# Last sparse feed-forward: paced scatters and gathers, earlier routing, expert tiles two shared batches later

## The reference, cut to what matters

```python
    def _L3_ffn_ref(x, w12, w3, router_w, expert_bias, sw1, sw2, sw3):
        g = x @ sw1.T
        u = x @ sw2.T
        shared_out = jax.nn.silu(g) * u @ sw3.T
        scores = jax.nn.sigmoid(x @ router_w.T)
        selection_scores = scores + expert_bias
        _, top_idx = jax.lax.top_k(selection_scores, TOPK)
        top_scores = jnp.take_along_axis(scores, top_idx, axis=-1)
        top_scores = top_scores / (top_scores.sum(-1, keepdims=True) + 1e-09)
...
        combine = jnp.zeros((T, E), x.dtype).at[jnp.arange(T)[:, None], flat_idx].add(flat_sc)
        h12 = jnp.einsum('td,ehd->teh', flat_x, w12)
        h1, h2 = jnp.split(h12, 2, axis=-1)
        h = jax.nn.silu(h1) * h2
        out_e = jnp.einsum('teh,edh->ted', h, w3)
        routed_out = jnp.einsum('ted,te->td', out_e, combine).reshape(b, s, d)
        return shared_out + routed_out
...
    x = x + jnp.tanh(g_ffn[3]) * _L3_ffn_ref(_layernorm(x, axis=-1), L3_ffn_w12, L3_ffn_w3, L3_ffn_router_w, L3_ffn_expert_bias, L3_ffn_sw1, L3_ffn_sw2, L3_ffn_sw3)
```

## Time and profile before

| | |
|---|---|
| timed runs | 2801.77, 2791.93, 2798.63 us; median 2798.63 us |
| profiled execution, its own time | 2822.25 us |
| span of its trace | 2820.5 us |
| mean granted TensorE clock | 0.933 of full speed |
| PE busy | 2371.5 us, 84% of the span |
| DVE, ACT, POOL busy | 1440.5, 1060.3, 602.9 us |

### The profile page before, as it was taken

One profiled execution on the slowest core, in us unless ns is written; L12 is line 12 of the kernel. 1 busy time (PEld: TensorE's weight loads), 2 busy tenths in 40 slices (PEclk: granted clock), 3 DMA queues, 4 the chain that ended last, 5 costly groups with the idle time before them and its releaser, 6 DMA issues. The chain is left out here.

```text
span 2820.5 us, 38098 instructions
## 1 busy us (share of the span) xinstructions
PE 2371.5 (84%) x10857; PEld 1472.6 (52%) x10884; DVE 1440.5 (51%) x3533; ACT 1060.3 (38%) x3280; POOL 602.9 (21%) x846
## 2 busy tenths in 40 slices
PE   4959999999788868868999999999444488877899
PEld 2436776677555434435666666666222255535675
DVE  4961111111245567745666566666577567762233
ACT  1022222122145435545555555555222255541232
POOL 3702222222123300003333333332000000003012
PEclk8959999999999989989999999999766699989999
DMA  7000000000300000000000000000200000021142
GB/s 286 0 7 6 6 6 6 6 6 6 130 5 0 0 3 0 0 6 1 1 0 0 0 0 0 0 0 0 106 0 0 3 5 4 4 76 47 58 128 64
DMA packets 40625, 68.83 MB, mean 24 GB/s; under 512 B 6752, under 2 KB 34400, under 8 KB 39264
## 3 DMA queue, kind: packets, MB, share of 16 engines
q1 hardware_dynamic: 37472, 59.44, 6.0%
q0 software_dynamic: 3072, 8.39, 0.9%
HBM read 51.30 MB, written 16.52 MB: 24 GB/s over the span
## 5 line engine op out<-in xcount | busy, mean ns | idle before, releaser
L808 DVE TENSOR_TENSOR moe_hid<-moe_act_g,moe_pU 128x384 f32<-128x384 f32 x128 | 70.9, 554 | 443.4 <-ACT moe_act_g L780 443.4
L780 ACT ACTIVATE moe_act_g<-moe_pG 128x384 f32<-128x384 f32 x128 | 62.8, 490 | 424.5 <-PE moe_pU L735 424.5
L714 POOL TENSOR_TENSOR moe_hidw<-moe_hid,moe_data_w_all 128x384 f32<-128x384 f32 x128 | 105.7, 826 | 426.7 <-DVE moe_hid L808 419.9
L1939 ACT ACTIVATE l2x_prob<-l2x_pS,l2x_nb,l2x_rms_q 128x256 f32<-128x256 f32 x256 | 142.5, 565 | 133.4 <-DVE l2x_nb L2087 133.4
L735 PE MATMUL moe_pG<-big,moe_xT 128*128 128x384 f32 x512 | 187.5, 489 | 4.1 <-POOL moe_xT L702 4.1
L756 PE MATMUL moe_pO<-big,moe_hT 128*128 128x256 f32 x768 | 186.8, 379 | 0.0
L735 PE MATMUL moe_pU<-big,moe_xT 128*128 128x384 f32 x512 | 186.3, 487 | 0.0
L967 PE MATMUL l2x_pQ<-big,l2x_xT 128*128 128x512 f32 x320 | 155.0, 607 | 13.7 <-POOL l2x_cT L2016 10.9
L756 PEld LDWEIGHTS moe_pO<-big,moe_hT 128*128 128x128 f32 x768 | 136.0, 190 | 13.2
L2084 DVE TENSOR_REDUCE l2x_negmax<-l2x_pS 128x2 f32<-128x512 f32 x128 | 87.8, 686 | 98.1 <-PE l2x_pS L1828 95.3
L735 PEld LDWEIGHTS moe_pU<-big,moe_xT 128*128 128x128 f32 x512 | 97.6, 191 | 68.3 <-issue 0.9
(11 more groups left out here) (454 smaller groups left out, 5230.4 us busy)
## 6 DMA issues: line engine op xcount, KB each, us to landing
route_x<-l3f_zero SPq DMA_DIRECT2D x1, 4992.0 KB, 16.7
l3f_xg<-route_x SPq DMA_DIRECT2D x39, 128.0 KB, 2.2
route_y<-l3f_y SPq DMA_DIRECT2D x39, 128.0 KB, 1.7
big<-in_f_gu SPq DMA_DIRECT2D x1, 4096.0 KB, 14.9
big<-in_e_gate SPq DMA_DIRECT2D x1, 3072.0 KB, 19.9
big<-in_e_up SPq DMA_DIRECT2D x1, 3072.0 KB, 20.6
big<-in_e_down SPq DMA_DIRECT2D x1, 3072.0 KB, 27.5
moe_lanes<-in_l2f_lanes SPq DMA_DIRECT2D x16, 192.0 KB, 2.8
```

The costliest lines, as they stand in the source:

```text
L714: pool.tensor_tensor(hidw[c % 2][:].rearrange("p (e i) -> p e i", e=n), hid[c % 2][:].rearrange("p (e i) -> p e i", e=n), bc(w, chunk // n ...
L1939: ins = act.activation(prob[g % 2][:, h, :], pS[j][:, (h % 2) * 2 * P:(h % 2 + 1) * 2 * P], ACT.Exp, scale=rms_q[g][:, h:h + 1], bias=nb[: ...
```

## The change

`EARLY` goes from 8 to 10, so 40 shared chunks stand ahead of the routed tiles (R0 = 40, R1 = 79) and 24 behind them. Each scatter now waits until PE has finished a given number of `up` items: 10 and one more for every one and a half scatters, 30 for the last. The two gathers of batch b wait for item number R1 + 1 + floor(1.5 b), capped at Q. The DVE adds the routed rows of batch b at item R1 + 4 + floor(1.5 b) instead of R1 + 4 + 2 b. Routing moves forward: batches 8 to 15 are normalised and turned in one group, the router products of 8 batches each stand at items 1 and 2 (before, of 4 batches each at items 2 to 5), Exp at item 3 (before 6), `route_scores` and `route_first` together at 3 (before 6 and 7), `route_second` at 4 (8), `ranks` at 5 (9), `route_slots` at 6 (10), `route_owners` at 7 (11), `route_weights` at 8 (12).

```diff
-    EARLY = B // 2
+    EARLY, PACE0 = 10, 10
...
-    group = {0: range(4, 8), 1: range(8, 12), 2: range(12, 16)}
+    group = {0: range(4, 8), 1: range(8, 16)}
...
             for b in range(B):
                 for k in range(TOPK):
+                    pool.wait_ge(gu_ps, PACE0 + 2 * (TOPK * b + k) // 3)
                     pool.indirect_dma_start(dx, bass.IndirectOffsetOnAxis(slot_i[:, k, b:b + 1], 0), nm.xn[b][:],
                                             None).then_inc(scattered, 16)
...
                 if b >= GR:
                     pool.wait_ge(combined, b - GR + 1)
+                pool.wait_ge(gu_ps, min(R1 + 1 + 3 * b // 2, Q))
...
-                if q in (2, 3, 4, 5):
-                    for b in range(4 * (q - 2), 4 * (q - 1)):
+                if q in (1, 2):
+                    for b in range(8 * (q - 1), 8 * q):
                         scores(b)
-                if q == 9:
+                if q == 5:
                     ranks()
...
-                if q == 6:
+                if q == 3:
                     act.wait_ge(logits, B)
...
-                return R1 + 4 + 2 * b
+                return R1 + 4 + 3 * b // 2
...
-                if q in (0, 1):
-                    for b in range(8 + 4 * q, 12 + 4 * q):
+                if q == 0:
+                    for b in range(8, 16):
                         nm.normalise(dve, b)
+                if q == 3:
+                    route_scores()
+                    route_first()
+                if q == 4:
+                    route_second()
                 if q == 6:
-                    route_scores()
+                    route_slots()
                 if q == 7:
-                    route_first()
+                    route_owners()
                 if q == 8:
-                    route_second()
-                if q == 10:
-                    route_slots()
-                if q == 11:
-                    route_owners()
-                if q == 12:
                     route_weights()
```

## The result

| | time | against the kernel before |
|---|---|---|
| before | 2797.01 us, median of 16 runs (2791.49 to 2802.22) | |
| after | 2803.32 us, median of 16 runs (2798.71 to 2808.75) | 1.0024, 95% interval 1.0015 to 1.0032 |

The changed kernel is 6.3 us slower. That is 0.24%: small, but sure. The forecast was 2797.4 us, 1.2 us under the median of its last timed runs. The profiled execution of the changed kernel took 2798.71 us, which is one of these 16 runs, where the one of before took 2822.25 and is not among its 16.

A forecast was written before the change was run, and what follows sets the result against it. PE was taken to pace the phase at 2.80 us per shared chunk, except for a stall during the scatters. Timed: 2798.63 - 5.9 (stall) + 2.2 (routing) + 1.5 (lumps) + 1.0 (combining) = 2797.4 us, range 2775 to 2806.

The forecast's parts named there:

- The stall's cause and place: Last phase, during the burst of 32 scatters: PE's reports come ever later, from some ten scatters on, costing 27.4 us when profiled.
- Step 1: Scatters paced by item waits, items 10 to 30: the scatter stall is gone, all 27.4 us gained in the profiled run.
- Profiled and timed runs: Profiled run 23.6 us above timed median: laid to per-instruction reports, so timed runs carry only a smaller stall, 5.9 us.
- S: The smaller scatter stall supposed in the timed runs, which the change removes: 5.9 us, bounds 0 and 29.5.
- Step 2: Routing in one chunk, first items: PE waits for DVE at the second product and at ranks, +2.2 us, bounds 1 and 3.5.
- Step 3: Transposes and router products in longer lumps: PE's clock drops earlier, slowing up(2) too, +1.5 us, bounds -1.6 and +4.1.
- rival 3: No stall in timed runs; up and two downs at 1.2 GHz after the lumps: 2807.4 us, slower; chance 0.07.
- Step 4: Gathers and combining at the end: small gather stall stays, +1.5 us in the profiled run; later combining adds +1.0 us.
- Rival 5: Scatter pace doesn't bite: a stalled PE holds scatters back too, or waits are already met; 2803 us; chance 0.07.
- Rival 1: Scatter stall is whole in the timed runs, so the change gains 21.2 us there: 2777.4 us; chance 0.28.

## Why the prediction was right or wrong

**The stall's cause and place: right.** It was read as lateness of PE's reports that grows with the scatters and begins some ten into the burst. The half burst, the missing scatters, and the paced and unpaced forms on chip A all bear it out. One thing stays open: the ends of PE's rows are modelled, so no trace tells whether the reports are late or the last writes of the work itself.

**Step 1, the pace ends the stall: right where there is one.** It removes 27.7 us on A, as the 27.4 of rows 3 said. The whole sum for the profiled run was 2801 us. The changed kernel was profiled at 2802.14 us on A.

**"Profiled and timed runs": this step failed.** The 23.6 us between the profiled execution and the timed median were explained by reports that only a profiled run sends, and S came out at 5.9 us. Neither holds. On A the timed runs carry the stall whole (27.9 us, scatters left out) and on B none of it (2804.08 against 2804.02 us, burst against pace). In the twelve experiments the profiled execution was at most 5.4 us above the slowest other run of the same kernel, and in nine of them among the others; it was never 20 above. The 23.6 us fit a profile from a chip of A's kind and timed runs from one of B's kind. The two medians of the kernel before there stand 30.4 to 32.8 us apart, but single runs spread over 7 to 13 us, so this fits without being shown. S should have been 0 or about 28, not 6. The 5.9 us were one execution less two stalls (2792.75) against a median (2798.63), and single runs of the kernel before spread over 10.7 us (2791.49 to 2802.22): from these numbers S couldn't be told from 0. The text had noted that the fastest timed run matches 2792.75, and called it maybe chance.

Beside this step stood the Trainium skill (Perfetto Trace Analysis, section Per-instruction lifecycle, Tensor Engine): the end shown for a matmul is an estimate, and the propagation of its counter lies outside the row. The page doesn't say whether a late report is the profiler's doing. The prediction's reading, that it can be real and so stand in timed runs too, is what A shows, with 27.9 us; on B nothing was late.

**Step 2, routing in one chunk: mechanism right, 1.6 us short.** The waits of PE are 0.80 + 1.41 = 2.2 us, 2.0 more than the 0.2 of before; the forecast had 2.4 and so +2.2. (Its sign, `ranks` 2 to 2.5 us after the start of the turning before them, came out as 1.82.) But behind these two waits came the low clock, 1.6 us, and that was not in the sum: 3.8 us in all, above the bound of 3.5. The kernel with `ranks` one item later gets 4.1 us back and shows the full clock there.

**Step 3, the lumps: right.** 1.7 us against 1.5, by the `up` named, the one at item 2. The upper bound of 4.1 doesn't follow from its rows, though: one `up` and two downs at the low level are 1.74 + 2 x 0.92 = 3.6 us, less the present 1.6 that is 2.0. Nor does the limit of +3.9 in rival 3: 8.4 less the other 4.7 is 3.7.

**Step 4: half right.** The combining costs 1.1 us against 1.0. The gathers' stall, supposed to stay with 1.5 us on top, is gone on A as well. POOL's timeline of the changed kernel there:

```profile
2746.20 0.95 POOL L2428 DMA_INDIRECT l3f_yk<-route_y,l3f_slot_i  x1 [0.30 <-issue]
2749.29 0.95 POOL L2428 DMA_INDIRECT l3f_yk<-route_y,l3f_slot_i  x1 [2.14 <-remote]
```

After ten gathers the eleventh waits 2.14 us. It needs the `up` of 2744.92, which ends at 2746.80, so the report of that `up` is some 2.5 us late, and the item wait holds POOL back by it. PE loses 0.14 us (2747.72 to 2750.66) where it lost 2.1 before. In the traces of A it is the same throughout: with the item waits of the gathers a chunk there loses at most 0.14 us (four kernels), without them PE loses 2.1 to 4.4 us (four kernels). That the waits do this, by ending the burst as soon as reports get late, fits but isn't shown alone: `EARLY` and the places of the combining differ too, and before the eleventh gather the kernel before also pauses, 1.96 us. Rival 5 had this thought for the case in which the pace would do nothing.

**The total.** Forecast -5.9 + 2.2 + 1.5 + 1.0 = -1.2 us; measured 0 + 3.8 + 1.7 + 1.1 = +6.6 against +6.3. Of the 7.5 us between forecast and result, 5.9 are S, 1.6 the clock behind `ranks`. Of the rivals, the third (no stall in timed runs, lumps at the low clock, 0.07) had the premise right and the price too high, 8.8; with 2.0 in place of its 4.1 it would have been 6.7, or 2805.3 us. Rival 5's 2803 us is the nearest time, by luck: its mechanism, waits that are met already, didn't happen. Rival 1 (the stall whole, 2777.4 us) is what happens on chip A in the difference, -24.5 us (21 to 29) against its -21.2, but from a base of 2828 us.

## What to carry to other kernels

- When a profiled execution stands far above the timed median, and the gap is about the size of one stall, ask first whether the two come from different chips. Here the stall was all there (A) or not there at all (B), and a share of it, as the forecast took it, was seen on neither.
- A long row of indirect transfers can be paced by a counter of the engine that it would disturb. Here that cost nothing that could be measured where there was no trouble (2804.02 against 2804.08 us) and gained 1% where there was. Such a wait also holds the row back when that engine's reports get late.
- Cost a wait of PE with what PE's clock does behind it: here 1.6 us on top of waits of 2.2 us. Small products were best spread here, 8 and not 32 in a row.

## What the runs showed of the hardware

- Back-to-back indirect scatters (0.96 us each, 0.30 apart) delayed what the other engines learn of PE's work, on one chip and not on another: 18.7 us for one `up` on A, 0.04 us for the same one on B. Why the chips differ, and what the scatters and PE's reports share, no run here tells. It isn't the speed of the transfers: in the burst form POOL issues them at 1.26 us and they move some 105 GB/s on both chips. The kernel before took 2822 us or more in all 38 runs beside others on A, and 2805.01 us or less in all 30 on B.
- The cost on A begins after about eleven scatters in a row; then each further one costs PE some 1.2 to 1.8 us (19 us for the last 16 of 32, 8.8 for the last 5 of 16). The scatters themselves don't get slower: on both chips the last of 32 takes POOL 0.96 us like the second. The Trainium skill (DMA: Bandwidth & Descriptors, section Anatomy of one DMA) says of the generation of descriptors that many can be emitted before the incremental cost shows up. For POOL's own time the traces agree, up to 32 scatters; what PE loses on A is another cost, of which that sentence doesn't speak.
